# First node pass of a graph network: the two norms of a turn share one inverse root, bias adds run during the power, transposes come first

## What is computed

```python
x  = (x - mean(x)) / sqrt(var(x) + 1e-5)     # first norm
h  = x @ w_in + b_in                         # projection
xn = (h - mean(h)) / sqrt(var(h) + 1e-5) * ln1_g + ln1_b
q, k, v = xn @ wq + bq, xn @ wk + bk, xn @ wv + bv
self_score = sum over each head of q * k     # the edge from a node to itself
```

## Time and profile before

| | |
|---|---|
| median of three runs | 4462.18 us (4457.46 to 4467.36) |
| span of the profiled execution | 4465.3 us |
| TensorE busy in the span | 82% |
| VectorE busy in the span | 72% |
| ScalarE busy | 38% |
| GpSimd busy | 46% |

### The profile page before, as it was taken

One profiled execution on the slowest core, in us unless ns is written; L12 is line 12 of the kernel. 1 busy time (PEld: TensorE's weight loads), 2 busy tenths in 40 slices (PEclk: granted clock), 3 DMA queues, 4 the chain that ended last, 5 costly groups with the idle time before them and its releaser, 6 DMA issues. The chain is left out here.

```text
span 4465.3 us, 82525 instructions
## 1 busy us (share of the span) xinstructions
PE 3681.2 (82%) x17048; PEld 2435.5 (55%) x17048; DVE 3232.5 (72%) x7299; ACT 1681.1 (38%) x4755; POOL 2072.2 (46%) x1938
## 2 busy tenths in 40 slices
PE   1777898888998857999988888888888758888488
PEld 1444555555555535777765555455555437777377
DVE  4777899888998865555548998898899766666501
ACT  0111555555555521222214555555555402222021
POOL 2113777777777730000007777777777500000022
PEclk8998999999999978999999999999999979999699
DMA  4224777777777731111117777777777512222011
GB/s 73 85 87 134 214 218 216 212 212 214 218 221 213 219 108 33 48 59 59 59 49 219 217 213 211 207 218 214 213 217 219 170 48 71 82 74 83 23 47 39
DMA packets 357834, 640.43 MB, mean 143 GB/s; under 512 B 107755, under 2 KB 199981, under 8 KB 357594
## 3 DMA queue, kind: packets, MB, share of 16 engines
q0 software_dynamic: 140144, 457.44, 34.7%
q1 hardware_dynamic: 217610, 182.03, 13.9%
HBM read 570.14 MB, written 69.95 MB: 143 GB/s over the span
## 5 line engine op out<-in xcount | busy, mean ns | idle before, releaser
L673 POOL DMA_INDIRECT edge_kv<-kv,edge_idx x1664 | 1871.0, 1124 | 542.1 <-issue 423.0
L852 PE MATMUL edge_sums<-edge_kv,edge_sel 128*128 128x272 f32 x3328 | 979.2, 417 | 142.0 <-ACT edge_sums L920 112.4
L805 PE MATMUL edge_q<-qc,edge_spread 128*128 x3328 | 921.3, 400 | 155.4 <-DVE edge_kv L715 130.4
L919 ACT COPY acc<-edge_sums x1664 | 641.2, 385 | 868.6 <-PE edge_sums L852 704.5
L805 PEld LDWEIGHTS edge_q<-qc,edge_spread 128*128 128x128 f32 x3328 | 580.6, 192 | 430.1 <-issue 374.6
L852 PEld LDWEIGHTS edge_sums<-edge_kv,edge_sel 128*128 128x128 f32 x3328 | 566.6, 190 | 441.8 <-issue 364.2
L715 DVE TENSOR_TENSOR edge_kv<-edge_kv,edge_q 128x512 f32<-128x512 f32 x832 | 564.7, 679 | 242.8 <-DMA edge_kv<-kv,edge_idx 227.2
L920 ACT COPY edge_sums<-edge_blank 128x272 f32 x1664 | 659.6, 396 | 0.0
L764 DVE TENSOR_TENSOR edge_kv<-edge_kv 128x512 f32<-128x512 f32 x832 | 564.4, 678 | 0.9 <-ACT edge_kv L909 0.9
L722 DVE TENSOR_REDUCE edge_score<-edge_kv 128x16 f32<-128x512 f32 x832 | 559.4, 672 | 0.2
L758 DVE TENSOR_TENSOR edge_sel<-cols,edge_tab 128x256 f32<-128x256 f32 x832 | 340.4, 409 | 0.0
(11 more groups left out here) (367 smaller groups left out, 3974.8 us busy)
## 6 DMA issues: line engine op xcount, KB each, us to landing
edge_rel<-step_rel SPq DMA_DIRECT2D x208, 256.0 KB
edge_kv<-kv,edge_idx POOLq DMA_INDIRECT x1664, 3.8
edge_flags<-step_flags SPq DMA_DIRECT2D x416, 32.0 KB
picked<-last_picked SPq DMA_DIRECT2D x25, 513.0 KB
kv<-first_kv_out SPq DMA_DIRECT2D x25, 512.0 KB
kv<-middle_kv_out SPq DMA_DIRECT2D x25, 512.0 KB
end_rows<-edge_ends SPq DMA_DIRECT2D x416, 8.5 KB
h<-first_h SPq DMA_DIRECT2D x25, 256.0 KB
```

The costliest lines, as they stand in the source:

```text
L673: nc.gpsimd.indirect_dma_start(kv[:, turn[0], j, 0:KV], None, dram["kv"], bass.IndirectOffsetOnAxis(ap=idx[:, turn[0], j:j + 1], axis=0)). ...
L805: mm = t.matmul(psq[m % QBUFS][:, j % 2, :], spread[:, turn[0] % 2, j * P:(j + 1) * P], qc[:, bass.ds(at[j % 2], D)], start=True, stop=True)
L852: pe_p.tick(t.matmul(psa[:, bass.ds(place[j % 2], QC)], sel[:, j, :], kv[:, turn[0], j, D:ROW], start=False, stop=True, skip_group_check=T ...
L919: s.copy(acc[:, bass.ds(at, QC)], psa[:, bass.ds(bank, QC)])
```

## The change

A function `first_pass` takes the place of `node_pass(nc, "first", ...)`. The instructions that compute are those of before, with three differences in order and shape. VectorE finishes the moments of x(t) and of h(t-1) and takes both through one root of four columns a lane (`var`, `minus_half`, `rs` and `yy` have `2 * W` columns: x in the first two, h in the last two). While GpSimd takes the power, VectorE does the adds of the first block of turn t-2 (`values(older, 0)`); those of the second follow behind the four normalisations. TensorE does both sets of transposes first, into PSUM tiles of their own (`pt_x`, `pt_h`), then the projection, then q/k/v, now of turn t-1 instead of t-2. The transposed and copied x (`xt`) and the normalised rows (`xn`, `hn`) have one buffer instead of two; `ht` has two.

```diff
+def first_pass(nc, a, dram, keep, weights):
...
+        @block.sync
...
+            def one(turn, b=None):
+                if exists(later(turn, 1)):
+                    load(later(turn, 1), first=b is not None and b < 1, final=b == TURNS - 2)
+                if exists(later(turn, -1)):
+                    lane = later(turn, -1)[0]
+                    dve_h.wait(sp, later(turn, -1), "h", beside=s_zero)
+                    sp.dma_start(rows_of(dram["h"], later(turn, -1)), h[:, lane, :, :]).then_inc(s_hout[lane], 16)
+                if exists(later(turn, -2)):
+                    lane = turn[0]
+                    dve_qkv.wait(sp, later(turn, -2), "kv1", beside=s_zero)
+                    sp.dma_start(rows_of(dram["kv"], later(turn, -2), slice(0, KV)), kv_out[:, lane, :, :])\
+                        .then_inc(s_kvout[lane], 16)
...
+        def columns(turn):
+            first = 0 if exists(turn) else W
+            return slice(first, 2 * W if exists(later(turn, -1)) else W)
...
+        @block.gpsimd
...
+                    dve_root.wait(pool, turn, "var", beside=s_zero)
+                    pool_root.tick(nc.gpsimd.tensor_tensor(rs[:, i, of], var[:, i, of], power[:, of], ALU.pow),
+                                   turn, "guess")
...
+        @block.vector
...
+            def stats(told, turn, i, rows, at):
+                for w in range(W):
+                    told.tick(v.bn_stats(out=st[:, i, at + w, :], in_=rows[:, w, :]), turn, f"stats{w}")
+
+            def moments(told, turn, i, at):
+                told.wait(dve, turn, f"stats{W - 1}", beside=s_weights)
+                for w in range(W):
+                    told.tick(v.bn_aggr(out=mv[:, i, at + w, :], in_=st[:, i, at + w, :]), turn, f"moments{w}")
+
+            def normed(told, turn, i, rows, into, at):
+                for w in range(W):
+                    told.tick(v.tensor_scalar(into[:, w, :], rows[:, w, :], mv[:, i, at + w, 0:1],
+                                              rs[:, i, at + w:at + w + 1], ALU.subtract, ALU.mult), turn, f"normed{w}")
+
+            def values(turn, w):
+                lane = turn[0]
+                q = qc[:, bass.ds(number(turn, W * D) + w * D, D)]
+                pe_h.wait(dve, turn, f"qkv{w}")
+                dve_qkv.tick(v.tensor_tensor(kv_out[:, lane, w, :], ph[w][:, D:3 * D], b_qkv[:, D:3 * D], ALU.add),
+                             turn, f"kv{w}")
+                dve_qkv.tick(v.tensor_tensor(q, ph[w][:, 0:D], b_qkv[:, 0:D], ALU.add), turn, f"q{w}")
+
+            def body(turn):
+                i, of = turn[0], columns(turn)
+                old, older = later(turn, -1), later(turn, -2)
+                root = exists(turn) or exists(old)
+                if exists(turn):
+                    landed(dve, s_x, turn)
+                    stats(dve_x, turn, i, x[:, i, :, :], 0)
+                if exists(old):
+                    stored_before(dve, s_hout, old)
+                    pe_x.wait(dve, old, "projected")
+                    dve_h.tick(v.tensor_tensor(h[:, old[0], :, :], pp[old[0]][:, :].rearrange("p (w d) -> p w d", w=W),
+                                               each(b_in[:, :]), ALU.add), old, "h")
+                if exists(turn):
+                    moments(dve_x, turn, i, 0)
+                if exists(old):
+                    dve_h.wait(dve, old, "h")
+                    stats(dve_h, old, i, h[:, old[0], :, :], W)
+                    moments(dve_h, old, i, W)
+                    dve_h.wait(dve, old, f"moments{W - 1}")
+                elif exists(turn):
+                    dve_x.wait(dve, turn, f"moments{W - 1}")
+                if root:
+                    dve_root.tick(v.tensor_scalar(var[:, i, of], mv[:, i, of, 1], EPS, None, ALU.add), turn, "var")
+                    dve_root.tick(v.tensor_scalar(minus_half[:, i, of], mv[:, i, of, 1], EPS, -0.5, ALU.add, ALU.mult),
+                                  turn, "minus_half")
+                if exists(older):
+                    stored_before(dve, s_kvout, older)
+                    values(older, 0)
+                if root:
+                    pool_root.wait(dve, turn, "guess")
...
+                if exists(turn):
+                    if exists(old):
+                        pe_x.wait(dve, old, "turned")
+                    normed(dve_x, turn, i, x[:, i, :, :], xn, 0)
+                if exists(old):
+                    if exists(older):
+                        pe_h.wait(dve, older, "turned")
+                    normed(dve_h, old, i, h[:, old[0], :, :], hn, W)
+                if exists(older):
+                    values(older, 1)
...
+        @block.tensor
...
+            def body(turn):
+                old, older, oldest = later(turn, -1), later(turn, -2), later(turn, -3)
+                if exists(turn):
+                    dve_x.wait(pe, turn, f"normed{W - 1}")
+                    if exists(old):
+                        act_x.wait(pe, old, "copied")
+                    turned(pe_x, turn, xn, pt_x)
+                if exists(old):
+                    dve_h.wait(pe, old, f"normed{W - 1}")
+                    if exists(older):
+                        act_h.wait(pe, older, "scaled1")
+                    turned(pe_h, old, hn, pt_h)
+                if exists(turn):
+                    if exists(older):
+                        dve_h.wait(pe, older, "h")
+                    act_x.wait(pe, turn, "copied")
+                    for w in range(W):
+                        for half in range(2):
+                            mm = t.matmul(pp[turn[0]][:, w * D:(w + 1) * D], rows_t(xt, half, w), w_in[:, half, :],
+                                          start=(half == 0), stop=(half == 1))
+                    pe_x.tick(mm, turn, "projected")
+                if exists(old):
+                    act_h.wait(pe, old, "scaled1")
+                    for w in range(W):
+                        if exists(older):
+                            dve_qkv.wait(pe, older, f"q{w}")
...
+        @block.scalar
...
+                if exists(turn):
+                    if exists(old):
+                        pe_x.wait(act, old, "projected")
+                    pe_x.wait(act, turn, "turned")
+                    act_x.tick(s.copy(xt[:, :], pt_x[:, :]), turn, "copied")
+                if exists(old):
+                    pe_h.wait(act, old, "turned")
...
-            node_pass(nc, "first", a, dram, keep, Weights(nc, held, "first", a, keep))
+            first_pass(nc, a, dram, keep, Weights(nc, held, "first", a, keep))
```

163 lines of the change are left out of this document (added).

## The result

The changed kernel takes 4389.15 us in the median of four runs (4385.7 to 4399.98), against 4464.77 for the kernel before in the runs beside it: a ratio of 0.9827 with a 95% interval of 0.9802 to 0.9851. A second set of runs gave 0.9838 (0.9802 to 0.9873). The profiled execution spans 4385.3 us.

What follows compares the result with a forecast made beforehand. VectorE's ordered list was taken to set the loop's 12.08 us turn. Removing 2.63 a turn over 20 turns gives 52.6, plus 4 at the ends: 56.6 us off the median 4462.18, so 4405.6 us, range 4394 to 4423.

Steps and rivals of the forecast that it cites:

- What bounds the kernel before: First pass's loop: VectorE's ordered list sets the 12.08 us turn: 8.94 work, 1.59 waits for the power, 1.55 short gaps.
- (a): VectorE's list in the loop: both waits for GpSimd's power go if the one left is covered, 1.59 us a turn.
- (d): VectorE's list: the two gaps in x's norm go, since other work now stands between, 0.21 us a turn.
- (b): VectorE's list: one variance/minus_half pair goes, 0.24 us a turn.
- (c): VectorE's list: one chain of three small steps goes with its handoffs, 0.59 us a turn.
- Added: VectorE's adds compute q's address per half and waits for TensorE move: taken as nothing, at most 0.46 us a turn.
- gaps that go with the waits: Case of a VectorE list shorter than counted, by 0.4 us a turn at the range's low end; chance 0.02.
- The power: GpSimd's four-column power taken as 0.69 us, at most 1.38; guess usable 1.04 after the variance's start, covered by the adds.
- the two engines might exclude each other: GpSimd's power could not run beside VectorE's adds: 0.7 us a turn, 17 us; part of a rival with chance 0.13.
- TensorE's order: Both transposes, projection, then q/k/v: 8.73 us a turn, the 1.19 us wait ahead of q/k/v gone, VectorE still setting the turn.
- Rival 2: TensorE becomes the loop's bound through q/k/v at a slower clock: 4415 to 4431 us; chance 0.08.
- Ends and queues: Turns outside the loop save 1.5 us ahead and 2.5 behind, 4 give or take 3; transfers at 111 GB/s charged nothing.

Runs made afterwards that it cites:

- the first run: The kernel before, first pass only, without VectorE's waits on its own last instruction after each norm and the self score: 11.24 us a turn, 4454.33 us in all.

## Why the prediction was right in its parts and wrong in its sum

- **What bounds the kernel before**: right. VectorE's list set the turn: three waits less on that list, and the turn is 0.84 us shorter.
- **Removed, (a) to (d)**: the price of the shared root held. Undone, (b) and (c), forecast at 0.83, cost 9.03 - 8.34 = 0.69 on VectorE's own list; that list then no longer has its 0.19 of waiting for the power, so the work itself is 0.88. Term (d), 0.21, was too small: with h's add behind x's statistics and x's moments behind that add, the waits on own results between them find something to run under. From x's statistics to its variance, and from h's add to h's statistics, the list of before took 1.21 (243.74 to 244.95) and 0.72 (247.44 to 248.16); the same steps now take 1.41 (240.21 to 241.62). From h's statistics to the variance it took 1.21, and now 1.10 (241.62 to 242.72). Together that is 0.63 less, not 0.21. The two rows of before that are not in the earlier trace rows:

```profile
248.16 0.75 DVE L1457 BATCH_NORM_STATS2 first_st<-first_h 128x6 f32<-128x256 f32 x2
...
249.37 0.17 DVE L1463 TENSOR_SCALAR first_var<-first_mv 128x2 f32<-128x2 f32 x1
```

- **The step that failed** is *Added*, with what stands ahead of it. The 1.55 us of short gaps in the old list were read in the rows, 0.33 of them were taken off with (c) and (d), and the other 1.22 priced as staying, as if they belonged to the instructions. The forecast saw the fewer waits and gave them a price of nothing; "gaps that go with the waits" had 2 in 100. The gap of 0.23 ahead of the reduction was read as address work, though its bracket in the earlier trace rows names VectorE's own product. What the runs showed in its place: a good part of these gaps belongs to the three waits on own results, and with the overlap that these forbid they were worth 0.84 us a turn in the kernel before. Put back into the changed kernel they cost 0.61 (8.95 - 8.34, both with 0.19 of waiting for the power).
- **The account of VectorE's list**, step by step and averaged over the loop, from the kernel before to the run with less work for TensorE: it went from 12.08 to 8.34, by 3.74 where 2.63 was forecast. The steps behind the three waits gave 0.82, where nothing was forecast. Term (d) gave 0.64, for 0.21. (a) and (b) gave 1.65, for 1.83, since 0.19 of waiting for the power stays on this list. (c) gave 0.50, for 0.59, since the step from the end of the Newton chain to the normalisation grew by 0.09. And 0.14 came from the steps to the product and to its reduction: in the loop of `node_pass` the waits there come with a second one (`beside=s_weights`), which the new function leaves out; no run undoes that by itself.
- **The power**: wrong in size, right in effect. Four columns took 1.01 us, between the two ends, so the guess is usable 1.36 us after the variance's start, later than the 1.21 at which the square could start. On VectorE's own list 0.2 us of waiting show (the run with less work for TensorE). In the changed kernel they don't, since TensorE holds the adds up by more. The cover is worth 9.305 - 8.447 = 0.86 us a turn. That the two engines might exclude each other falls: a power takes 1.01 us beside the adds (at 243.03), and 1.01 with VectorE at rest, ahead of the loop:

```profile
106.76 1.01 POOL L1878 TENSOR_TENSOR first_rs<-first_var,first_power 128x4 f32<-128x4 f32 x1 [10.48 <-DVE first_minus_half L1935]
```

  The rule of the Trainium skill ("SBUF — State Buffer", section "SBUF: two separate sides"), by which adds from PSUM with one SBUF input leave the shared ports free, agrees with these two rows.
- **TensorE's order**: right. Undone by itself it costs 1.85 us a turn (10.298 - 8.447), more than any other part; the sum of pitches written down ahead of that run was 10.3.
- **Rival 2**, TensorE becomes the bound, came true by another way than forecast: not through a slow clock, which stood at 1.00, but because VectorE's list fell to TensorE's 8.33. It takes 0.1 us a turn of the gain.
- **Ends and queues**: 4.5 us for 4, which is in part luck: 2.2 ahead of the loop where 1.5 was forecast, 2.3 behind it for 2.5. At 124 GB/s the loop's table has no wait for a transfer.

How the price of the three waits divides can be read in the kernel before. Its written-out turns have the same waits, but with constants for values and addresses and no branch. From the normalisation of x to h's add, and from the reduction to the next instruction:

```profile
379.25 0.74 DVE L1472 TENSOR_SCALAR first_xn<-first_x,first_mv,first_rs 128x256 f32<-128x256 f32 x2
...
380.02 0.69 DVE L1497 TENSOR_TENSOR first_h<-first_pp,first_b_in 128x512 f32<-128x512 f32 x1
...
386.86 0.69 DVE L1511 TENSOR_REDUCE self<-first_tmp 128x16 f32<-128x512 f32 x1
...
387.58 0.69 DVE L1497 TENSOR_TENSOR first_h<-first_pp,first_b_in 128x512 f32<-128x512 f32 x1
```

These steps take 0.77 and 0.72, and the one behind h's normalisation 0.77 (383.38 to 384.15). In the first run's loop, without the waits, they take 0.65, 0.60 and 0.65: the lost overlap is 0.12 each, 0.36 in all. In the loop of the kernel before they take 0.90, 1.00 and 0.81 in the mean, so the other 0.45 goes with what only the loop has, the register work and the branch. That these are what fills it is inferred; no row lists them.

## What to carry to other kernels

On VectorE here, a gap of 0.1 to 0.6 us behind a wait for the engine's own last result was a price of that wait, not of the instruction: count such waits on the engine that sets the time, and drop those that guard nothing or put independent work between. On an engine that waits for another anyway they cost nothing, as in the middle pass here. And when a list is shortened below the next engine's, what is left of the gain is read from that engine's busy time, here 8.33 of 8.45.

## What the runs showed of the hardware

GpSimd's power grows by 0.16 us a column, from 0.69 us for 128 x 2 to 1.01 for 128 x 4, where VectorE's small steps stay at 0.16 in all. Two VectorE instructions without a wait between them overlap by 0.08 to 0.1 us; a wait on the own result costs 0.12 us at least, and 0.5 (with the waits put back) to 0.7 (kernel before) where a loop turns back behind it. The Trainium skill ("VectorE: DVE Perf Modes", section "The DRAIN you can't avoid") measured no extra cost for a semaphore behind every operation; here the runs show one, 0.84 us a turn for three waits in the loop, and 0.12 for each where the turns are written out.
